# A decoder layer on one core: the cross-attention's slots regrouped, its softmax and rope steps rewritten

## Chip, cores, metric

One Trainium2 chip, one of its cores. The metric is the device time of one execution in microseconds (us), as the median of the runs. Engines: TensorE (PE, with its weight loads as PEld), VectorE (DVE), ScalarE (ACT), GpSimd (POOL), SyncE (SP, which here issues the DMAs).

## The reference, cut to what matters

The kernel computes a decoder layer for x of 64 sequences x 64 tokens x 256: causal self-attention with 16 heads, cross-attention to a context, a quantised feed-forward part, each added to x and followed by a layer norm. The change lies in the cross-attention (b = 64, lq = lk = 64, H = 16, HD = 128, R = 64):

```python
kv_c = kv @ W_kvc                      # 64 wide
q_c = q @ W_dq                         # 96 wide
q_nope = (q_c @ W_uq).reshape(b, lq, H, HD)
q_rope = _rope((q_c @ W_qr) ..., lq)   # 64 per head
k_nope, v = (kv_c @ W_uk) ..., (kv_c @ W_uv) ...
k_rope = _rope(kv_c @ W_kr, lk)
scores = (q_nope . k_nope + q_rope . k_rope) * scale
good = (k_ids <= qs) & (k_ids >= qs - LOOKBACK)
attn = softmax(where(good, scores, NEG))
return (attn @ v).reshape(b, lq, H * HD) @ W_o
```

with `_rope(x) = concat(x1*cos - x2*sin, x1*sin + x2*cos)` over the two halves of a head's 64 numbers.

## The kernel before

The 4096 tokens are handled as NT = 8 tiles of TILE = 512 (BT = 8 sequences of T = 64); the heads in HP = 8 pairs. Four blocks follow each other: self-attention (written out in full), `prepare_cross` (8 tiles; the normalised x, q_c as `qc`, the keys `kh`, kv_c by tokens as `KV`, and the weights folded so that the scores are a product of 64 + 64 numbers per head: a latent part and a rope part), the cross-attention loop, and the feed-forward part. X, the residual, stays in SBUF.

The cross-attention loop runs 64 slots, one for each head pair g and tile j: the helper `slots` writes the first 8 out, loops over the head pairs 1 to 7 with the 8 tiles inside, and adds seven slots to drain. The pair is the outer loop, the tile the inner one. Each engine has its own program; in slot n it does step k for item n - lag, `has(lag)` says whether that item exists, and semaphores join the engines. Operands are split for precision: a product of f32 numbers is three bf16 products (PASSES: high*high, high*low, low*high); the high half is read in place from the f32 tile, the low half is made by a subtraction on GpSimd or VectorE.

What a slot does, by item:

- TensorE, L889: `qP[0..2] = WQ[k].T @ qc`, 3 x 3 matmuls of 512 columns: the latent part, the rope part, and the rope part with its halves swapped (a third set of weight columns, from `in_qrs`).
- ScalarE, L934: latent part of two heads, scaled, into `qh` rows 0 to 63. VectorE, L990: `turn[0] = qP[1]*cos`, `turn[1] = qP[2]*sin`; L997: `qh` rows 64 to 127 = turn[0] + turn[1], one instruction of 64 rows for each head.
- GpSimd, L1019: `qhl`, the low half of `qh`. TensorE, L882: scores `sP`, 24 matmuls of 64 columns.
- VectorE, L983: `scores = sP + mask` (f32 mask in SBUF); L985: row maxima, negated. ScalarE, L943: eight exponentials of 64 columns, each with its row's bias and its sum.
- VectorE, L968: reciprocals of the sums; GpSimd, L1008: probs * inverse. TensorE, L896: four transposes; ScalarE, L948: `probsT` (f32).
- TensorE, L903: `oP = KV.T @ probsT`, four f32 matmuls of 128 columns. ScalarE, L928: four copies to `oT`, which bring the 64-row parts of the two heads to their rows. GpSimd, L1012: `oTl`, its low half.
- TensorE, L912: projection with `WB`, 12 matmuls of 256 columns; VectorE, L973: projP + X into X, in every slot. In the slots after the last item VectorE also takes the statistics of the 32 row blocks for the next layer norm (L542), and ScalarE sums the absolute ffn weights (L956), which SyncE loads at the loop's start (L868).

The order of work on VectorE in a slot is: reciprocal, addition into X, mask addition, maximum, two products, two sums.

The lines of the page that name L205 to L517 belong to the self-attention; `mask_of` (L389) and `square_of_tile` (L487) in it make the cross-attention's mask ahead of time, L572 is the normalisation of one block of 128 tokens in the preparation, L790 makes the low half of a folded weight there.

## Time and profile before

| | us |
|---|---|
| three runs | 1627.15, 1627.86, 1629.86; median 1627.86 |
| the profiled execution's own time | 1630.34 |
| its span, first to last instruction | 1628.5 |
| self-attention | 0 to 976 |
| preparation of the cross-attention | 976 to 1049 |
| cross-attention loop | 1049 to 1452.3 |
| quantisation, then the feed-forward loop | 1452.7 to 1492, then to 1628.5 |

Busy over the whole span: PE 1487.4 us (91%), PEld 1083.8 (67%), DVE 1322.9 (81%), ACT 1334.4 (82%), POOL 1231.7 (76%). The mean granted clock of TensorE is 0.971 of 2.4 GHz. DMA moves 36.92 MB, most of it in the first 50 us and around the preparation; there is none in most of the loop.

How to read the profile: a timeline gives instructions in order of time, neighbours of one kind merged ("x4"), with the idle time of the engine ahead of an instruction and what ended it in brackets. Two starts that lie closer than the first one's duration mean that instructions overlap in the engine's pipeline. A group by line gives the count, total and mean of a kind of instruction.

### The profile page before, as it was taken

The numbers are of one execution on the slowest core, as the hardware profiler recorded it, in microseconds if no ns is written. First come the engines' busy times: TensorE is split into PE (matmuls) and PEld (weight loads), VectorE is DVE, ScalarE is ACT, GpSimd is POOL, SyncE is SP. The second block draws the span as 40 slices with busy tenths as digits, with TensorE's granted clock in tenths as the row PEclk, the third lists the DMA queues.
The fourth block names the chain that finished last, engine by engine and source line by source line (L and its number), as shares of the span: only waits on it lengthen the run. The fifth ranks groups of instructions, "written<-read, shape, count | busy, mean of one in ns | idle before, by whom it ended". The sixth has DMA issues, their size and how long they took to land. (4 is left out here: it accounts for less than half of the span.)

```text
span 1628.5 us, 54216 instructions
## 1 busy us (share of the span) xinstructions
PE 1487.4 (91%) x20018; PEld 1083.8 (67%) x20018; DVE 1322.9 (81%) x2913; ACT 1334.4 (82%) x4174; POOL 1231.7 (76%) x1147
## 2 busy tenths in 40 slices
PE   6998999999999999999999968799999999845996
PEld 3666777777777777777777755366666666633664
DVE  3887777777777777777777778699999999967986
ACT  5877888888888888888888856599999999976664
POOL 5999888888898898898898846466666666611787
PEclk9999999999999999999999978999999999976999
DMA  6700000000000000000000002200000000000011
GB/s 222 191 2 15 16 3 15 16 15 3 15 15 3 16 15 5 13 15 15 3 15 3 3 2 68 86 3 2 0 0 0 0 0 0 0 1 0 14 39 53
DMA packets 27066, 36.92 MB, mean 23 GB/s; under 512 B 8288, under 2 KB 19872, under 8 KB 26848
## 3 DMA queue, kind: packets, MB, share of 16 engines
q1 hardware_dynamic: 26848, 33.99, 6.6%
q8 instruction: 140, 2.29, 0.5%
q14 instruction: 78, 0.64, 0.1%
HBM read 29.79 MB, written 4.19 MB: 21 GB/s over the span
## 5 line engine op out<-in xcount | busy, mean ns | idle before, releaser
L420 DVE SCALAR_TENSOR_TENSOR X<-projP,r,X 128x256 f32<-128x256 f32 x512 | 211.3, 476 | 2.5 <-PE projP L254 2.4
L234 PEld LDWEIGHTS svP<-W,xT 128*128 128x128 bf16 x3072 | 182.7, 98 | 31.4 <-issue 1.4
L205 PE MATMUL qkssP<-xT,W 128*128 128x512 bf16 x768 | 190.4, 384 | 13.5 <-POOL W L485 11.1
L480 POOL TENSOR_TENSOR y_sql<-y_sq 128x512 bf16<-128x512 f32 x128 | 133.0, 1039 | 80.5 <-ACT y_sq L321 80.1
L234 PE MATMUL svP<-W,xT 128*128 128x128 bf16 x3072 | 192.9, 219 | 0.7 <-issue 0.7
L205 PE MATMUL kP<-xT,W 128*128 128x512 bf16 x768 | 188.4, 382 | 0.0
L254 PE MATMUL projP<-W,y 128*128 128x256 bf16 x1024 | 177.1, 275 | 3.2 <-POOL yl L480 3.2
L943 ACT ACTIVATE x_probs<-x_scores,x_ntop 128x64 f32<-128x64 f32 x512 | 170.0, 335 | 7.4 <-DVE x_ntop L985 7.4
L336 ACT ACTIVATE probs<-scores,ntop 128x64 f32<-128x64 f32 x512 | 170.5, 339 | 1.9 <-DVE ntop L410 1.9
L1008 POOL TENSOR_TENSOR x_probs<-x_probs,x_inv 128x512 f32<-128x512 f32 x64 | 66.7, 1042 | 107.9 <-DVE x_inv L968 107.9
L480 POOL TENSOR_TENSOR k_sql<-k_sq 128x512 bf16<-128x512 f32 x128 | 133.1, 1040 | 19.8 <-ACT k_sq L341 19.2
L254 PE MATMUL projP<-W,yl 128*128 128x256 bf16 x512 | 140.9, 275 | 0.0
L889 PE MATMUL xq<-qc,WQ 128*128 128x512 bf16 x576 | 136.5, 383 | 3.8 <-PEq L661 2.9
L514 POOL TENSOR_TENSOR ql<-q 128x512 bf16<-128x512 f32 x128 | 139.0, 1086 | 0.0
L480 POOL TENSOR_TENSOR q_sql<-q_sq 128x512 bf16<-128x512 f32 x128 | 133.0, 1039 | 7.6 <-ACT q_sq L328 7.6
L205 PEld LDWEIGHTS kP<-xT,W 128*128 128x128 bf16 x768 | 75.7, 99 | 92.2 <-issue 2.8
L517 POOL TENSOR_TENSOR vl<-v 128x512 bf16<-128x512 f32 x128 | 135.7, 1060 | 0.0
L480 POOL TENSOR_TENSOR yl<-y 128x512 bf16<-128x512 f32 x128 | 133.0, 1039 | 0.0
L450 DVE TENSOR_TENSOR ptl<-pyP,pth 128x256 bf16<-128x256 f32 x128 | 54.3, 424 | 96.8 <-ACT pth L355 96.8
L997 DVE TENSOR_TENSOR qh<-turn 64x512 f32<-64x512 f32 x128 | 128.6, 1005 | 3.1
L1019 POOL TENSOR_TENSOR qhl<-qh 128x1024 bf16<-128x1024 f32 x64 | 121.1, 1893 | 6.2 <-DVE qh L997 6.2
L433 DVE COPY v<-svP 128x512 f32<-128x512 f32 x128 | 88.4, 691 | 44.9 <-PE svP L234 44.1
(190 smaller groups left out, 4829.1 us busy)
## 6 DMA issues: line engine op xcount, KB each, us to landing
w_stage<-in_wqkvp SPq DMA_DIRECT2D x16, 512.0 KB, 3.5
x_stage<-in_xT SPq DMA_DIRECT2D x8, 512.0 KB, 3.6
...
okv<-in_wgT SPq DMA_DIRECT2D x1, 1024.0 KB, 4.9
okv<-in_wuT SPq DMA_DIRECT2D x1, 1024.0 KB, 7.2
```

The costliest lines, as they stand in the source:

```text
L205: last = nc.tensor.matmul(dst[:, :], weight(parity, u, i, c), xT[:, z, c, tok], start=(c == 0 and k == 0), stop=(c == CC - 1 and k == 2))
L234: last = nc.tensor.matmul(svP[:, b * D:(b + 1) * D], xT[:, u, c, t * TILE + b * P:t * TILE + (b + 1) * P], weight(parity, z, 2, c), start= ...
L254: last = nc.tensor.matmul(projP[:, b * C:(b + 1) * C], y_part, W[:, (j - 3) // NT % 2, z, 3 * CC * D:], start=(i == 0), stop=(i == 2))
L336: last = nc.scalar.activation(probs[:, b, :], scores[:, b, :], ACT.Exp, bias=ntop[:, b:b + 1], accum_out=total[:, b:b + 1])
L420: last = nc.vector.scalar_tensor_tensor(acc, projP[:, b * C:(b + 1) * C], r[:, PB + b:PB + b + 1], acc, ALU.mult, ALU.add)
L480: return nc.gpsimd.tensor_tensor(dst[:, :], src[:, :], high(src, slice(None), 0, TILE), ALU.subtract)
L514: nc.gpsimd.tensor_tensor(ql[:, j % 2, :], q[:, j % 2, :], high_of(q, j % 2), ALU.subtract).then_inc(s_ql, 1)
L517: nc.gpsimd.tensor_tensor(vl[:, j % 4, :], v[:, j % 4, :], high_of(v, j % 4), ALU.subtract).then_inc(s_vl, 1)
L889: last = nc.tensor.matmul(qP[k][:, :], at(WQ[:, u, :, k], g), qc[:, z, j * TILE:(j + 1) * TILE], start=(i == 0), stop=(i == 2))
L943: last = nc.scalar.activation(probs[:, s, b, :], scores[:, b, :], ACT.Exp, bias=ntop[:, b:b + 1], accum_out=total[:, b:b + 1])
L997: last = nc.vector.tensor_tensor(qh[KVC:P, j % 2, :, i, :], turn[rows, 0], turn[rows, 1], ALU.add)
L1019: nc.gpsimd.tensor_tensor(qhl[:, s, :], flat, flat.bitcast(BF16)[:, 1::2], ALU.subtract).then_inc(s_ql, 1)
```

## The change

- The loop is written out in full and turned round: the tile is the outer loop, the head pair the inner one. The projections of a tile's eight pairs add up in PSUM (`start` only at g == 0), so `projP + X` runs once per tile; the row statistics of a tile follow in the next tile's slots.
- The third set of rope weights and its matmuls go. VectorE multiplies the rope part by -sin or sin (`turn`), SyncE moves its four blocks of 32 rows to the partner rows by four SBUF-to-SBUF DMAs (`turned`), VectorE multiplies the PSUM tile by cos in place and one slot later adds the two into `qh`. `qh` has three buffers, rope PSUM two.
- The mask is bf16 and is added by TensorE: one matmul with the identity of 512 columns opens the bank, the 24 score matmuls accumulate on it. To make the bf16 mask, self-attention uses an f32 scratch of two tiles.
- Softmax: VectorE takes the maximum from `sP`, subtracts it (`shifted`), ScalarE does one exponential of 512 columns, VectorE sums it.
- Transposed probabilities are split in bf16 (`pth` by ScalarE, `ptl` by VectorE), `KV` too (its low half by two more VectorE instructions per tile in the preparation); P times V is 12 bf16 matmuls.
- ScalarE takes `oP` to `oA` in one copy; four DMAs bring its parts to their rows (`oB`); GpSimd makes `oBl`.
- The ffn weights are loaded in slots 8 to 10. `in_ctxT` is laid out on the host so that a tile's two halves stand apart. ScalarE's load of its function table at the loop's start goes.

The diff, cut to its core:

```diff
-                m = late["mask"][:, i * BT:(i + 1) * BT, :]
                 dve.wait_ge(late["s_square"], 2 * i + 2)
-                nc.vector.tensor_scalar(m, m, (LOOKBACK / 2) ** 2, NEG, ALU.is_gt, ALU.mult)
+                nc.vector.tensor_scalar(late["mask"][:, i * BT:(i + 1) * BT, :], late["square"][:, i % 2], (LOOKBACK / 2) ** 2, NEG,
+                                        ALU.is_gt, ALU.mult).then_inc(late["s_mask"], 1)
...
-                m = late["mask"][:, i * BT:(i + 1) * BT, :]
+                m = late["square"][:, i % 2]
                 pool.wait_ge(late["s_segf"], 1)
+                wait(pool, late["s_mask"], i - 1)
...
+                if 0 <= t < NT:
+                    dve.wait_ge(s_KV, t + 1)
+                    tk, own_ = tkP[:, 0:PB * KVC].rearrange("p (b k) -> p b k", b=PB), slice(t * PB, (t + 1) * PB)
+                    nc.vector.tensor_tensor(KV[0:T, 1, own_, 0:KVC], tk[0:T], KV[0:T, 0, own_, 0:KVC], ALU.subtract)
+                    nc.vector.tensor_tensor(KV[T:P, 1, own_, KVC:P], tk[T:P], KV[T:P, 0, own_, KVC:P], ALU.subtract).then_inc(s_KVl, 1)
...
+    N = NT * HP
+    S_AT, T_AT, PV_AT, PROJ_AT = 3, 4, 5, 7
...
+            for n in range(N + PROJ_AT):
+                m = n - PV_AT - 1
+                if has(n, PV_AT + 1):
+                    wait(sp, s_oe, m + 1)
+                    wait(sp, s_proj, m - 1)
+                    for par in range(2):
+                        for i in range(2):
+                            sp.dma_start(oB[i * KVC:(i + 1) * KVC, m % 2, par * HT:(par + 1) * HT],
+                                         oA[par * KVC:(par + 1) * KVC, m % 2, i, :]).then_inc(s_ot[m % 2], 16)
+                if has(n, 0):
+                    wait(sp, s_turn, n + 1)
+                    wait(sp, s_qh, n - 1)
+                    half = R // 2
+                    for r in range(0, P, half):
+                        o = r + half if r % R == 0 else r - half
+                        sp.dma_start(turned[o:o + half, n % 2, :], turn[r:r + half, n % 2, :]).then_inc(s_swap[n % 2], 16)
+                if 8 <= n < 11:
+                    ffn_weights(n - 8, ("wgT", "wuT", "wdT")[n - 8])
...
+                if has(n, S_AT):
+                    m = n - S_AT
+                    tile, s = m // HP, m % 3
+                    wait(pe, s_ql, m + 1)
+                    wait(pe, s_shifted, m)
+                    nc.tensor.matmul(sP[:, :], identb[:, :], mask[:, tile * BT:(tile + 1) * BT, :].rearrange("p b t -> p (b t)"),
+                                     start=True, stop=False)
                     flat = qh[:, s].rearrange("p b i t -> p (b i t)")
                     for b in range(BT):
+                        first = tile * TILE + b % PB * P + b // PB * T
                         for i, (u, z) in enumerate(PASSES):
                             q_part = flat[:, b * P:(b + 1) * P].bitcast(BF16)[:, 1::2] if u == 0 else qhl[:, s, b * P:(b + 1) * P]
+                            last = nc.tensor.matmul(sP[:, b * T:(b + 1) * T], q_part, kh[:, z, first:first + T], start=False, stop=(b == BT - 1 and i == 2))
                     last.then_inc(s_s, 1)
...
+                if has(n, 0):
+                    tile, g = n // HP, n % HP
+                    for k, dst, done in ((1, ropeP[n % 2], s_ropeP), (0, latP, s_latP)):
+                        if k == 1:
+                            wait(pe, s_qh, n - 1)
+                        else:
+                            wait(pe, s_lat, n)
                         for i, (u, z) in enumerate(PASSES):
+                            last = nc.tensor.matmul(dst[:, :], WQ[:, u, g, k], qc[:, z, tile * TILE:(tile + 1) * TILE], start=(i == 0), stop=(i == 2))
+                        last.then_inc(done, 1)
...
+                if has(n, PV_AT):
+                    m = n - PV_AT
+                    wait(pe, s_ptl, m + 1)
+                    wait(pe, s_oe, m)
                     for b in range(PB):
                         for i, (u, z) in enumerate(PASSES):
+                            last = nc.tensor.matmul(oP[:, b * P:(b + 1) * P], KV[:, u, m // HP * PB + b, :], (pth, ptl)[z][:, m % 2, b * P:(b + 1) * P],
+                                                    start=(i == 0), stop=(i == 2))
+                    last.then_inc(s_o, 1)
+                if has(n, T_AT):
+                    m = n - T_AT
+                    wait(pe, s_norm, m + 1)
+                    wait(pe, s_ptl, m)
+                    for b in range(PB):
+                        last = nc.tensor.transpose(ptP[:, b * P:(b + 1) * P], probs[:, m % 2, b].rearrange("p q s -> p (q s)"), ident[:, :])
+                    last.then_inc(s_pt, 1)
...
+                if has(n, PROJ_AT):
+                    m = n - PROJ_AT
+                    g = m % HP
+                    wait(pe, s_ol, m + 1)
+                    if g == 0:
+                        wait(pe, s_acc, m // HP)
+                    for b in range(PB):
+                        for i, (u, z) in enumerate(PASSES):
+                            o_part = oB[:, m % 2, b * P:(b + 1) * P].bitcast(BF16)[:, 1::2] if u == 0 else oBl[:, m % 2, b * P:(b + 1) * P]
+                            last = nc.tensor.matmul(projP[:, b * C:(b + 1) * C], o_part, WB[:, z, g], start=(g == 0 and b % 2 == 0 and i == 0),
+                                                    stop=(g == HP - 1 and b % 2 == 1 and i == 2))
                     last.then_inc(s_proj, 1)
...
+                if has(n, S_AT):
+                    m = n - S_AT
+                    wait(act, s_shifted, m + 1)
+                    wait(act, s_pt, m - 1)
+                    nc.scalar.activation(probs[:, m % 2].rearrange("p b q s -> p q b s"), shifted[:, m % 2].rearrange("p (q b) s -> p q b s", q=2),
+                                         ACT.Exp).then_inc(s_exp, 1)
+                if has(n, T_AT):
+                    m = n - T_AT
+                    wait(act, s_pt, m + 1)
+                    wait(act, s_o, m - 1)
+                    nc.scalar.activation(pth[:, m % 2, :], ptP[:, :], ACT.Copy).then_inc(s_pth, 1)
+                if has(n, 0):
+                    wait(act, s_latP, n + 1)
+                    wait(act, s_s, n - 2)
                     for i in range(2):
+                        last = nc.scalar.activation(qh[0:KVC, n % 3, :, i, :], latP[i * KVC:(i + 1) * KVC, :].rearrange("p (b t) -> p b t", b=BT),
                                                     ACT.Copy, scale=SCALE)
                     last.then_inc(s_lat, 1)
+                if has(n, PV_AT):
+                    m = n - PV_AT
+                    wait(act, s_o, m + 1)
+                    wait(act, s_ot[m % 2], 64 * (m // 2))
+                    nc.scalar.activation(oA[:, m % 2].rearrange("p i (b t) -> p b i t", b=PB), oP[:, :].rearrange("p (b i t) -> p b i t", b=PB, i=2),
+                                         ACT.Copy).then_inc(s_oe, 1)
...
+            for n in range(N + PROJ_AT):
+                if has(n, T_AT):
+                    m = n - T_AT
+                    wait(dve, s_exp, m + 1)
+                    nc.vector.tensor_reduce(total[:, :], probs[:, m % 2].rearrange("p b q s -> p (b q) s"), AX, ALU.add).then_inc(s_sum, 1)
+                    wait(dve, s_sum, m + 1)
+                    wait(dve, s_norm, m)
                     nc.vector.reciprocal(inv[:, :], total[:, :]).then_inc(s_inv, 1)
+                if has(n, PV_AT):
+                    m = n - PV_AT
+                    wait(dve, s_pth, m + 1)
+                    wait(dve, s_o, m - 1)
+                    nc.vector.tensor_tensor(ptl[:, m % 2, :], ptP[:, :], pth[:, m % 2, :], ALU.subtract).then_inc(s_ptl, 1)
+                if has(n, S_AT):
+                    m = n - S_AT
+                    wait(dve, s_s, m + 1)
+                    nc.vector.tensor_reduce(top[:, :], by_token(sP[:, :]), AX, ALU.max).then_inc(s_top, 1)
+                    wait(dve, s_top, m + 1)
+                    wait(dve, s_exp, m - 1)
+                    nc.vector.tensor_tensor(shifted[:, m % 2], by_token(sP[:, :]), top[:, :].unsqueeze(2).to_broadcast([P, BT, T]),
+                                            ALU.subtract).then_inc(s_shifted, 1)
+                if has(n, 0):
+                    wait(dve, s_ropeP, n + 1)
+                    wait(dve, s_swap[n % 2], 64 * (n // 2))
+                    nc.vector.tensor_tensor(by_token(turn[:, n % 2]), by_token(ropeP[n % 2][:, :]), tabs[:, 1, :].unsqueeze(1).to_broadcast([P, BT, T]),
+                                            ALU.mult).then_inc(s_turn, 1)
+                if has(n, 1):
+                    m = n - 1
+                    wait(dve, s_swap[m % 2], 64 * (m // 2 + 1))
+                    wait(dve, s_cos, m + 1)
+                    wait(dve, s_s, m - 2)
                     for i in range(2):
                         rows = slice(i * R, (i + 1) * R)
+                        last = nc.vector.tensor_tensor(qh[KVC:P, m % 3, :, i, :], by_token(ropeP[m % 2][rows, :]), by_token(turned[rows, m % 2]), ALU.add)
                     last.then_inc(s_qh, 1)
+                if has(n, 0):
+                    wait(dve, s_turn, n + 1)
+                    rope = by_token(ropeP[n % 2][:, :])
+                    nc.vector.tensor_tensor(rope, rope, tabs[:, 0, :].unsqueeze(1).to_broadcast([P, BT, T]), ALU.mult).then_inc(s_cos, 1)
+                if has(n, PROJ_AT):
+                    m = n - PROJ_AT
+                    tile, g = m // HP, m % HP
+                    if g == HP - 1:
+                        wait(dve, s_proj, m + 1)
+                        acc = X[:, tile * PB:(tile + 1) * PB, :]
+                        nc.vector.tensor_tensor(acc, projP[:, :].rearrange("p (b c) -> p b c", b=PB), acc, ALU.add).then_inc(s_acc, 1)
+                    if tile >= 1 and 1 <= g < 1 + PB:
+                        wait(dve, s_acc, tile)
+                        next_norm.statistics((tile - 1) * PB + g - 1)
+            wait(dve, s_acc, NT)
+            for b in range(PB):
+                next_norm.statistics((NT - 1) * PB + b)
...
+            for n in range(N + PROJ_AT):
+                if has(n, T_AT):
+                    m = n - T_AT
+                    wait(pool, s_inv, m + 1)
+                    p_ = probs[:, m % 2].rearrange("p b q s -> p (b q) s")
                     nc.gpsimd.tensor_tensor(p_, p_, inv[:, :].unsqueeze(2).to_broadcast([P, BT, T]), ALU.mult).then_inc(s_norm, 1)
+                if has(n, PROJ_AT):
+                    m = n - PROJ_AT
+                    wait(pool, s_ot[m % 2], 64 * (m // 2 + 1))
+                    wait(pool, s_proj, m - 1)
+                    nc.gpsimd.tensor_tensor(oBl[:, m % 2, :], oB[:, m % 2, :], oB[:, m % 2, :].bitcast(BF16)[:, 1::2], ALU.subtract).then_inc(s_ol, 1)
+                if has(n, 1):
+                    m = n - 1
+                    wait(pool, s_lat, m + 1)
+                    wait(pool, s_qh, m + 1)
+                    wait(pool, s_s, m - 2)
+                    flat = qh[:, m % 3].rearrange("p b i t -> p (b i t)")
+                    nc.gpsimd.tensor_tensor(qhl[:, m % 3, :], flat, flat.bitcast(BF16)[:, 1::2], ALU.subtract).then_inc(s_ql, 1)
```

## Rows read from the trace of the kernel before

**Rows 1.** Busy us in the loop's middle: PE, PEld, DVE, ACT, POOL; granted clock, DMA share, GB/s

```profile
1085.00:1415.00 330.00, 310.19 (x3181) 220.75 (x3180) 323.67 (x446) 324.73 (x1286) 218.95 (x168) 1.00 0.00 0
```

**Rows 2.** Timeline of DVE over one slot: start us, duration us, then the instruction

```profile
1200.81 0.20 DVE L968 RECIPROCAL x_inv<-x_total 128x8 f32<-128x8 f32 x1
1200.92 1.17 DVE L973 TENSOR_TENSOR X<-xprojP,X 128x1024 f32<-128x1024 f32 x1
1202.02 0.68 DVE L983 TENSOR_TENSOR x_scores<-xsP,mask 128x512 f32<-128x512 f32 x1
1202.73 0.69 DVE L985 TENSOR_REDUCE x_ntop<-x_scores 128x8 f32<-128x512 f32 x1
1203.33 1.28 DVE L990 TENSOR_TENSOR turn<-xq,tabs 128x512 f32<-128x512 f32 x2
1204.65 1.34 DVE L997 TENSOR_TENSOR qh<-turn 64x512 f32<-64x512 f32 x1
1206.01 0.69 DVE L997 TENSOR_TENSOR qh<-turn 64x512 f32<-64x512 f32 x1
1206.73 0.20 DVE L968 RECIPROCAL x_inv<-x_total 128x8 f32<-128x8 f32 x1
```

**Rows 3.** Timeline of POOL in the same slot

```profile
1201.09 1.04 POOL L1008 TENSOR_TENSOR x_probs<-x_probs,x_inv 128x512 f32<-128x512 f32 x1 [1.56 <-DVE x_inv L968]
1203.56 1.89 POOL L1019 TENSOR_TENSOR qhl<-qh 128x1024 bf16<-128x1024 f32 x1
```

**Rows 4.** Timeline of ACT in the same slot

```profile
1200.94 1.53 ACT L928 ACTIVATE oT<-xoP 64x256 f32<-64x256 f32 x4
1202.51 1.20 ACT L934 ACTIVATE qh<-xq 64x512 f32<-64x512 f32 x2
1203.60 0.34 ACT L943 ACTIVATE x_probs<-x_scores,x_ntop 128x64 f32<-128x64 f32 x1
1206.37 0.60 ACT L948 ACTIVATE x_probsT<-xptP 128x512 f32<-128x512 f32 x1
```

**Rows 5.** Timeline of PE in the same slot, with idle time before and its releaser

```profile
1200.30 2.11 PE L889 MATMUL xq<-qc,WQ 128*128 128x512 bf16 x9
1202.68 1.08 PE L903 MATMUL xoP<-x_probsT,KV 128*128 128x128 f32 x8
1205.51 0.23 PE L882 MATMUL xsP<-kh,qh 128*128 128x64 bf16 x2 [0.37 <-POOL qhl L1019]
```

**Rows 6.** Group of instructions by line, whole span: count, busy us, mean ns, idle before

```profile
L402 DVE TENSOR_TENSOR svP<-svP,rk 128x256 f32<-128x256 f32 x128 | 54.3, 424 | 3.8 <-PE svP L280 3.8
```

**Rows 7.** DMA issues with KB and us to landing; timeline of SyncE's queue, two issues

```profile
okv<-in_wdT SPq DMA_DIRECT2D x1, 1024.0 KB, 9.6
tabs<-in_rope SPq DMA_DIRECT2D x1, 96.0 KB, 2.1
...
54.28 1.45 SPq L189 DMA_DIRECT2D kvf<-in_L_xattn_W_kvc  x1
56.92 0.43 SPq L189 DMA_DIRECT2D uqT<-in_uqT  x1
```

**Rows 8.** Timeline of DVE in the preparation, with its idle time and releaser

```profile
987.18 4.95 DVE L572 TENSOR_SCALAR X<-X,ln_mean,ln_rstd 128x256 f32<-128x256 f32 x4
1012.89 0.69 DVE L790 TENSOR_TENSOR WB<-fold,WB 128x512 bf16<-128x512 f32 x1 [0.53 <-ACT WB L760]
1014.10 3.10 DVE L572 TENSOR_SCALAR X<-X,ln_mean,ln_rstd 128x256 f32<-128x256 f32 x4
```

**Rows 9.** Timeline of DVE at the loop's start and end

```profile
1050.52 1.34 DVE L990 TENSOR_TENSOR turn<-xq,tabs 128x512 f32<-128x512 f32 x2 [3.02 <-PE xq L889]
1065.30 0.20 DVE L968 RECIPROCAL x_inv<-x_total 128x8 f32<-128x8 f32 x1
...
1421.30 4.02 DVE L542 BATCH_NORM_STATS2 ln_stats<-X 128x6 f32<-128x256 f32 x12
1450.91 1.41 DVE L542 BATCH_NORM_STATS2 ln_stats<-X 128x6 f32<-128x256 f32 x4
```

199 lines of the change are left out of this document (51 added, 148 removed).

## Prediction, before the change was run

> **What bounds the kernel now.** I read the busy table by stretch first: it shows which stage the change lives in and which engine is full there. In the cross-attention loop VectorE is busy 323.7 of 330 us and ScalarE 324.7, TensorE 310 and GpSimd 219, and TensorE's granted clock is 1.00 [rows 1]. Two engines are full, so the second reading is one slot (one head pair of one tile of 512 tokens) on each engine, as a timeline. On VectorE [rows 2] the reader is to see that each instruction starts where the one before it ends, or a little earlier, and that the reciprocal of one slot stands 5.92 us behind that of the last (1200.81 to 1206.73): 64 slots of this are 379 us. Two of its 5.92 us are the sum of the rope products, L997: the first of the pair takes 1.34, the second 0.69. The first one starts at 1204.65, while GpSimd's `qhl` runs from 1203.56 to 1205.45 [rows 3], and it ends 0.54 after that. So about 0.65 us of each slot is waiting for GpSimd. The instructions that read one operand from PSUM show nothing of the kind: the addition into X takes 1.17 beside GpSimd's `x_probs` [rows 2, 3], and the two rope products 1.28 together beside `qhl`. L997 alone reads two operands from SBUF. The Trainium skill's page "SBUF — State Buffer", section "Who interferes with whom", has it as a rule: a VectorE instruction with two SBUF inputs and a GpSimd instruction that reads SBUF wait for each other, one with a single SBUF input does not. By that rule L997 costs 0.7 once its GpSimd neighbour is out of the way, as the trace also has it.
>
> ScalarE [rows 4] is full for another reason: eight exponentials of 64 columns, each with the read-out of its sum, run from 1203.60 to 1206.37, 2.77 us, and the four parts of `oT` take 1.53. TensorE comes third and waits 0.37 for `qhl` at each slot's start [rows 5].
>
> **The change, engine by engine.** Durations overlap on VectorE, so I count from start to start. An instruction of 512 columns with a PSUM operand, or a reduction, takes 0.60 when its follower doesn't need it (1202.73 to 1203.33), and 0.71 when it does (1202.02 to 1202.73); X costs 1.09, the reciprocal 0.12 [rows 2].
>
> VectorE per slot, new order: sum of the exponentials, whose follower needs it, 0.72; reciprocal 0.12; `ptl` 0.60 (the nearest row, a subtraction from PSUM with bf16 output, L790, lasts 0.69 as the others do [rows 8]); maximum 0.72; subtraction 0.60; sine product 0.60; two sums into `qh` 1.20, since both now read one operand from PSUM; cosine product, back into PSUM, 0.60 (L402 writes to PSUM, lasts 0.42 for 256 columns [rows 6], on the same line as 0.69 for 512). Together 5.16. The maximum is taken from PSUM, which no row shows; its bounds are 0.60 (reduction from SBUF) and, if a PSUM source adds what it could at most add to a copy, about 0.80; I take 0.72. The addition into X now comes once in eight slots, and four row statistics with it: (1.09 + 4 x 0.335)/8 = 0.30, the statistics from twelve in 4.02 us [rows 9]. That makes 5.46 on average against 5.92.
>
> ScalarE: one exponential of 512 columns. A copy of that shape, L948, takes 0.60 [rows 4]; the eight small ones take 2.77. `oA` is one instruction of 0.60 too, instead of 1.53. The rest stays: 0.60 + 0.60 + 1.20 + 0.60 = 3.0 of a slot. It leaves the bound.
>
> TensorE: three of the nine wide matmuls go (the nine last 2.11 [rows 5], 0.23 each, so 0.7 less); one mask matmul of 512 columns comes (0.23); P times V goes from four f32 products in 1.08 [rows 5] to twelve bf16 ones of 128 columns, a quarter of a wide one each, 0.7. From 5.55 (5.92 less the 0.37 wait) to some 4.7.
>
> GpSimd: unchanged, two instructions of 1.04 and one of 1.89, 4.0 [rows 3]. But `qhl` of head pair n-1 now waits for the sums of the same slot, at 4.6 into it, so GpSimd runs into the next slot. I followed the ring: sums end at 4.6, `qhl` at 6.6, normalisation 7.6, `oBl` 8.6, projection on TensorE 10.1, mask and scores 11.2; the maximum that reads these scores is due at 2 x 5.16 + 1.45 = 11.8. It holds with 0.6 to spare.
>
> **The DMA detour** is what the old trace doesn't show. The swap of slot n leaves when the sine product ends, 3.4 into the slot, and the sums of the next slot want it 5.1 later. SyncE issues four transfers, about 0.48 each (issue rows run from 0.43 to 1.45 [rows 7] as the queue is free or not); the last lands 2.1 after its issue (96 KB from HBM [rows 7]). 3 x 0.48 + 2.1 + 0.2 for the two signals = 3.7. Bounds: 3.0 (issues at their shortest and a quicker landing from SBUF) and 4 x 1.45 + 2.1 = 7.9. I take 3.7, since the queue carries only 0.5 MB per slot. Then the cover is 1.4 us. Eight issues at 0.48 fill 3.8 us of SyncE's slot. The four `oT` transfers wait for ScalarE's last step of the slot before; behind that wait on SyncE stands the swap, which isn't due for another 3 us. If the cover is gone, each microsecond costs half a microsecond per slot, because a sine product waits for the sums two slots back: 2T = 5.54 + L, with L the detour and 5.54 VectorE's work between. T = 5.46 holds up to L = 5.4.
>
> **Sum.** Fill: the first rope matmuls no longer stand beside a third set, but 0.3 behind `identb`, so the first sine product comes at 1050.3 (it was 1050.52 [rows 9]); the swap lands 3.7 after its end, at 1054.7, and the sums and the cosine product close slot 1 at 1056.7. Slot 2 waits for a rope matmul (0.8, since its PSUM tile is freed by these sums) and adds 1.9 of VectorE, to 1059.4; slot 3 has the maximum and the subtraction besides, to 1063.1. So slot 4 begins at 1063, against 1065.3 [rows 9]. From there 60 slots: 60 x 5.16, seven additions into X and 24 statistics, 309.6 + 15.7 = 325, so slot 64 begins at 1388.5; before, at 1419.9 (36 slots after 1206.73). Drain: in order, the last three heads go through exponential, transposition, P times V, the `oT` detour (3.7), `oBl`, projection, X (1.2) and four statistics (1.4): 29 us, end 1417.5, where the loop before ended at 1452.3 [rows 9]. That is 34.8 less. The ffn weights, three transfers of 1 MB, now stand among the swaps of slots 8 to 10; 1.5 MB per slot against 9.6 us for 3 MB [rows 7] just about fits: +1.
>
> Preparation before the loop: two subtractions of 64x256 per tile, 0.7 us on VectorE, stand where it idles 0.53 ahead of a fold, L790 [rows 8], in most tiles; left over are 0.1 to 0.5 a tile, +1.2. `qrs` goes, and with it a GpSimd subtraction beside which four normalisations lasted 4.95 instead of 3.10 [rows 8]: -1.9. Bounds of the whole preparation: -2 and +5.6 (nothing hidden); I take -0.7. The mask now goes through two small tiles; its extra wait names a step two tiles back and costs nothing, at most 8 x 0.1 if late. The other stages are untouched.
>
> In all -34.8 + 1.0 - 0.7, about -34: the profiled execution's own time of 1630.3 becomes 1596.3. The median of the runs lies 2.5 below that execution, so 1594.
>
> **Rivals.** (a) The cover of a ring is thinner than I make it: the swap lands at 6.0, or `qhl` and what hangs on it take 1.3 us more per two slots. T becomes 5.6 to 5.8, +9 to +22 us: 1603 to 1616. For it: the ring over GpSimd has 0.6 of slack only, and signals between engines are counted at 0.1. Against: X and the statistics stretch VectorE's slots, not these rings. (b) Slower: the eight small transfers don't keep up. Price: if an issue takes 1.1 us (the row of 1.45 is such a one), SyncE needs 8.8 us per slot, 60 x 3.3 = +200, 1794; if it is the landing, L = 7.9 gives T = 6.7, +75, 1669. It decides from L = 6.5, or from 0.75 us per issue; from there the kernel is slower than before. Against: an issue beside an idle queue is 0.43 to 0.6. The Trainium skill's "SBUF — State Buffer", section "The DMA setup-cost knee", warns of just this pattern, a loop of transfers of 64 KiB, and gives it about 138 GB/s; by that, as an estimate, 0.5 MB would take 3.8 us of each slot and still fit. No row of this trace shows a transfer from SBUF to SBUF. (c) The gain is hidden: VectorE's new instructions are slower by what ends the overlap (0.70 instead of 0.60, as two SBUF operands show), eight of them, +0.8: T = 6.2, less 0.3 for what overlaps still, so 5.9, and the time stays within a few microseconds, 1625. Against: none reads two SBUF operands.
>
> **How the numbers follow.** Forecast 0.66, (a) 0.20, (b) 0.08, (c) 0.06. The forecast's own range is 1586 to 1603: VectorE's slot may be 0.1 off either way (6 us) and fill, drain and preparation 3. With (a) taken in, the range is 1584 to 1618. A measurement of this kernel tells 0.2%, 3.3 us, from no change. Faster: 0.66 + 0.20 and half of (c), 0.89; same 0.02; slower 0.09.
>
> **What would show it.** In the changed profile: two reciprocals 5.2 apart in most slots, 6.2 where X is added; VectorE over 97% busy in the loop, both sums into `qh` at 0.68 beside GpSimd; ScalarE some 3 us per slot, the one exponential 0.6; TensorE idle 0.5 to 0.8 per slot at clock 1.0; the swap landing 3.7 after its product. I am wrong if VectorE idles ahead of the sums (DMA) or of the maximum (GpSimd's ring), if the maximum from PSUM lasts over 0.8, or if TensorE's clock falls with its new idle time.

## The result, and the profile after

The changed kernel takes 1625.1 us (median of 16 runs, 1621.3 to 1629.1) against 1628.75 for the kernel before, measured beside it (16 runs): a ratio of 0.9971, 95% interval 0.9961 to 0.9981. It is faster, by 0.3%, where 2.1% was forecast. The profiled execution of the changed kernel took 1624.4 us of its own, span 1622.7, and was forecast at 1596.3.

First the page's busy table for the whole span, then the busy table by stretch for the loop's middle (PE, PEld, DVE, ACT, POOL; granted clock, DMA share, GB/s), which answers to [rows 1].

```profile
PE 1426.3 (88%) x19943; PEld 1055.6 (65%) x20146; DVE 1311.8 (81%) x3001; ACT 1136.4 (70%) x3021; POOL 1228.8 (76%) x1146
...
1081.00:1400.00 319.00, 269.62 (x3140) 192.22 (x3193) 308.61 (x519) 151.03 (x272) 212.25 (x163) 1.00 0.41 101
```

VectorE (DVE) is busy 308.6 of 319 us. ScalarE (ACT), full before, is down to 151. GpSimd ran 163 instructions, three a slot, so a slot takes 319 x 3/163 = 5.87 us on average, the share of X and its statistics included. Before, a slot took 5.92, its addition into X included [rows 2].

One slot of the changed kernel on VectorE, ScalarE, GpSimd and SyncE's queue, from timelines (start us, duration us, the instruction, in brackets the idle time before it and who ended it). These answer to [rows 2 to 4].

```profile
1207.33 0.69 DVE L1010 TENSOR_REDUCE x_total<-x_probs 128x8 f32<-128x512 f32 x1
1208.05 0.20 DVE L1013 RECIPROCAL x_inv<-x_total 128x8 f32<-128x8 f32 x1
1208.17 0.65 DVE L1018 TENSOR_TENSOR x_ptl<-xptP,x_pth 128x512 bf16<-128x512 f32 x1
1208.74 0.68 DVE L1022 TENSOR_REDUCE x_top<-xsP 128x8 f32<-128x512 f32 x1
1209.45 0.69 DVE L1025 TENSOR_TENSOR x_shifted<-xsP,x_top 128x512 f32<-128x512 f32 x1
1210.06 0.68 DVE L1030 TENSOR_TENSOR x_turn<-xropeP,tabs 128x512 f32<-128x512 f32 x1
1210.77 1.39 DVE L1039 TENSOR_TENSOR qh<-xropeP,x_turned 64x512 f32<-64x512 f32 x2
1212.20 0.70 DVE L1044 TENSOR_TENSOR xropeP<-xropeP,tabs 128x512 f32<-128x512 f32 x1
1212.93 0.69 DVE L1010 TENSOR_REDUCE x_total<-x_probs 128x8 f32<-128x512 f32 x1
...
1210.18 0.63 ACT L972 ACTIVATE x_probs<-x_shifted 128x512 f32<-128x512 f32 x1 [2.78 <-DVE x_shifted L1025]
1210.71 0.58 ACT L978 ACTIVATE x_pth<-xptP 128x512 bf16<-128x512 f32 x1
1211.19 1.18 ACT L983 ACTIVATE qh<-xlatP 64x512 f32<-64x512 f32 x2
...
1206.70 1.89 POOL L1078 TENSOR_TENSOR qhl<-qh 128x1024 bf16<-128x1024 f32 x1 [1.93 <-issue]
1208.55 1.04 POOL L1066 TENSOR_TENSOR x_probs<-x_probs,x_inv 128x512 f32<-128x512 f32 x1
1209.55 1.04 POOL L1071 TENSOR_TENSOR oBl<-oB 128x512 bf16<-128x512 f32 x1
...
1205.17 2.45 SPq L903 DMA_DIRECT2D x_turned<-x_turn  x4
1207.72 2.46 SPq L895 DMA_DIRECT2D oB<-oA  x4
```

VectorE is back to back, as forecast, but the slot from L1010 to L1010 is 5.60 us and not 5.16. Counted from start to start, up to the sine product every step is what the sum said, within 0.03: 0.72, 0.12, 0.57, 0.71, 0.61. Then four starts are late: sine product to first sum 0.71, first to second sum 0.70 (the pair lasts 1.39), second sum to cosine product 0.73, cosine product to the next slot's L1010 0.73. The sum had 0.60 for each, 2.40; they take 2.87. That is 0.47 too much; the other steps give 0.03 back, and 0.44 is left.

ScalarE, GpSimd and SyncE all have slack: ScalarE waits 2.78 us for `x_shifted`, GpSimd 1.93 ahead of `qhl`. SyncE has the least: counted issue by issue from 1081 to 1380, the idle stretches of its queue that are longer than 0.15 us add up to 22.4 us of 299, 0.4 us a slot. VectorE's wait for the swap in these 319 us, from the table of waits, and the two new transfers in the table of DMA issues (KB, median us to landing):

```profile
DVE qh L1039 <- DMA x_turned<-x_turn: 0.9, 2, 0.6
...
x_turned<-x_turn SPq DMA_DIRECT2D x256, 64.0 KB, 2.0
oB<-oA SPq DMA_DIRECT2D x256, 64.0 KB, 2.0
```

The loop's start and its end on VectorE, which answer to [rows 9]:

```profile
1048.03 0.69 DVE L1030 TENSOR_TENSOR x_turn<-xropeP,tabs 128x512 f32<-128x512 f32 x1 [2.73 <-PE xropeP L933]
...
1414.19 0.69 DVE L1010 TENSOR_REDUCE x_total<-x_probs 128x8 f32<-128x512 f32 x1
...
1443.50 1.23 DVE L1051 TENSOR_TENSOR X<-xprojP,X 128x1024 f32<-128x1024 f32 x1 [12.23 <-PE xprojP L960]
1444.76 1.40 DVE L543 BATCH_NORM_STATS2 ln_stats<-X 128x6 f32<-128x256 f32 x4
```

Slot 4 begins at 1062.3 (forecast 1063), slot 64 at 1414.2 (1388.5), the loop ends at 1446.2 (1417.5). So 60 slots took 351.9 us instead of 325, and this is where the gain went. The drain is 32.0 instead of 29.

### The profile page after: what moved, and what is told of

Same layout as the page of the kernel before. It is cut to its first block and busy times, and to the rows that moved or that the text cites. A ratio compares the mean times of both kernels' runs of the same rounds, so it can differ in the third digit from the quotient of the medians.

```text
span 1622.7 us, 53246 instructions
## 1 busy us (share of the span) xinstructions
PE 1426.3 (88%) x19943; PEld 1055.6 (65%) x20146; DVE 1311.8 (81%) x3001; ACT 1136.4 (70%) x3021; POOL 1228.8 (76%) x1146
## 5 line engine op out<-in xcount | busy, mean ns | idle before, releaser
L205 PE MATMUL qkssP<-xT,W 128*128 128x512 bf16 x641 | 160.9, 382 | 33.6 <-issue 20.3
L972 ACT ACTIVATE x_probs<-x_shifted 128x512 f32<-128x512 f32 x64 | 40.3, 630 | 191.4 <-DVE x_shifted L1025 191.4
L450 DVE TENSOR_TENSOR ptl<-pyP,pth 128x256 bf16<-128x256 f32 x128 | 54.3, 424 | 96.8 <-ACT pth L355 96.8
L205 PEld LDWEIGHTS qkssP<-xT,W 128*128 128x128 bf16 x768 | 64.9, 98 | 81.5 <-issue 12.3
L407 DVE SCALAR_TENSOR_TENSOR scores<-svP,r,bias 128x64 f32<-128x64 f32 x512 | 110.0, 278 | 4.5
L960 PE MATMUL xprojP<-WB,oB 128*128 128x256 bf16 x512 | 89.2, 276 | 25.5 <-POOL oBl L1071 25.5
```

What stands on the lines that cost most here:

```text
L205: last = nc.tensor.matmul(dst[:, :], weight(parity, u, i, c), xT[:, z, c, tok], start=(c == 0 and k == 0), stop=(c == CC - 1 and k == 2))
L407: last = nc.vector.scalar_tensor_tensor(scores[:, b, :], svP[:, b * T:(b + 1) * T], r[:, b:b + 1], row, ALU.mult, ALU.add)
L960: last = nc.tensor.matmul(projP[:, b * C:(b + 1) * C], o_part, WB[:, z, g], start=(g == 0 and b % 2 == 0 and i == 0), stop=(g == HP - 1 an ...
```

## The experiments

The question is why four starts in each slot are 0.10 to 0.13 late. Theory A: a VectorE instruction overlaps the tail of the one in front of it only if it starts at the partitions that were last used in that memory, for reading and for writing. (A memory here is SBUF or PSUM.) The rivals are B, the waits and the transfer ahead of the sums; C, the 64-row shape or the output in PSUM; D, GpSimd at the port. Behind each measured time stands its ratio to the kernel before, measured beside it, with the 95% interval; the changed kernel's is 0.9971. The kernel before took 1628.75 to 1632.5 from one series to the next, so versions of different series are compared by these ratios.

**The sums turned round.**

```
-                    for i in range(2):
+                    for i in (1, 0):
```

> The changed kernel with one thing turned round: of a slot's two 64-row sums, the one that reads rows 64 to 127 is issued first. Work, tiles, waits and engines are the same. Theory A (a VectorE instruction does not overlap the one in front of it when it starts to read PSUM, to read SBUF or to write SBUF at another partition than was last used there): in the changed kernel four starts of a slot pay, the first sum (output from row 64), the second (inputs from row 64), the cosine product (inputs back at row 0) and the instruction behind it (SBUF output back at row 0): 0.71, 0.70, 0.73 and 0.73 us from start to start, where other 512-element instructions take 0.57 to 0.61. Turned round, the second sum ends on rows 0 to 63, where the cosine product reads: it should start 0.60 to 0.62 us behind the sum instead of 0.73, the slot fall from 5.60 to 5.48, the kernel by 64 x 0.12 = 7 to 8 us, ratio to the kernel before 0.992 to 0.993. The Trainium skill, VectorE: DVE Perf Modes, section Two Vector instructions with no wait between them, has this as its condition for a held instruction. Theory B (three waits ahead of the sums, or the transfer that feeds them), theory C (a 64-row instruction or one that writes PSUM costs more in itself) and theory D (GpSimd's traffic at the same port): the order changes nothing, slot 5.60, ratio 0.997.

Measured: 1618.8 us, 0.9933 (0.9913 to 0.9953). VectorE's timeline:

```profile
1204.29 0.68 DVE L1030 TENSOR_TENSOR x_turn<-xropeP,tabs 128x512 f32<-128x512 f32 x1
1205.00 1.39 DVE L1039 TENSOR_TENSOR qh<-xropeP,x_turned 64x512 f32<-64x512 f32 x2
1206.32 0.68 DVE L1044 TENSOR_TENSOR xropeP<-xropeP,tabs 128x512 f32<-128x512 f32 x1
1207.03 0.69 DVE L1010 TENSOR_REDUCE x_total<-x_probs 128x8 f32<-128x512 f32 x1
...
1212.50 0.69 DVE L1010 TENSOR_REDUCE x_total<-x_probs 128x8 f32<-128x512 f32 x1
```

The pair still lasts 1.39, but the cosine product starts 1.32 behind it instead of 1.43; the slot is 5.47. Nothing but the order differs, so of the rivals none explains it; a 64-row sum isn't slow in itself, since the second one now holds its follower for 0.61 only. 6 us are won by letting the second sum end where the next instruction reads.

**The sums on all 128 rows** (their result left out from the fourth slot on).

```
+                            last = nc.vector.tensor_tensor(late["square"][:, :].rearrange("p i b t -> p (i b t)").rearrange("p (b i t) -> p b i t", b=BT, i=2)[:, :, i, :], by_token(ropeP[m % 2][:, :]), by_token(turned[:, m % 2]), ALU.add)
```

> The changed kernel, but from the fourth slot on the two sums are made on all 128 rows, from row 0, into a tile that nobody reads, so the rope part of the queries keeps old values: the result of the sums is left out, not their work. Each sum still has 512 elements a row, the same waits and the same order. Theory A (starting partition): no instruction of the slot leaves row 0, so the two sums, the cosine product and what follows it all start 0.58 to 0.61 us behind the one before; the slot goes from 5.60 to 5.16 us and the kernel from 1625 to about 1597 us (61 slots x 0.44 = 27 us), the time forecast, ratio about 0.980. Theory B (waits or the transfer): the first sum still starts 0.71 behind the sine product, slot 5.5 at best. Theory C: with the 64-row shape as the cause both sums take 0.60 but the cosine product, which has 128 rows in both kernels, still 0.73 if its PSUM output is what costs there: slot 5.3, 1607 us. Theory D (GpSimd at the port): sums unchanged at 0.70, slot 5.60, 1625 us.

Measured: 1603.7 us, 0.9837 (0.9812 to 0.9863).

```profile
1209.10 0.68 DVE L1030 TENSOR_TENSOR x_turn<-xropeP,tabs 128x512 f32<-128x512 f32 x1
1209.70 1.28 DVE L1042 TENSOR_TENSOR square<-xropeP,x_turned 128x512 f32<-128x512 f32 x2
1210.89 0.69 DVE L1047 TENSOR_TENSOR xropeP<-xropeP,tabs 128x512 f32<-128x512 f32 x1
1211.49 1.21 DVE L1054 TENSOR_TENSOR X<-xprojP,X 128x1024 f32<-128x1024 f32 x1
...
DVE square L1042 <- DMA x_turned<-x_turn: 8.4, 11, 1.8
```

All four starts are at 0.60: 0.60, 1.19 for the pair, 0.60. Where nobody waits, one reciprocal follows another by 5.11 (1113.84 to 1118.95), so the forecast's 5.16 was the slot of a kernel that never leaves row 0. The elements a row and the waits are the same, and the cosine product still writes PSUM: B, D and that half of C fall. From 1075 to 1385 the first sum starts 0.59 to 0.60 behind the sine product in 38 of 58 slots, and later in the others, of which the table of waits puts 11 down to the swap. So 21 us come back and not 27: the last line, from the table of waits, has 8.4 us of VectorE waiting for the swap, against 0.9 in the changed kernel. SyncE's queue is full here: its idle stretches over 0.15 us add up to 1.7 us of 299, and a round of eight issues takes 5.53 us on average. The average slot, X's share included, can't be shorter than that here.

**The three waits moved ahead of the sine product.**

```
+                if has(n, 1):
+                    wait(dve, s_swap[(n - 1) % 2], 64 * ((n - 1) // 2 + 1))
+                    wait(dve, s_cos, n)
+                    wait(dve, s_s, n - 3)
                 if has(n, 0):
                     wait(dve, s_ropeP, n + 1)
```

> The changed kernel with the three waits of the two sums (for the transfer, for the cosine product of the slot before and for the buffer) moved ahead of the sine product, so that nothing stands between the sine product and the sums. Theory A (starting partition): the starts stay at 0.71, 0.70, 0.73 and 0.73 us, slot 5.60, time within 1 us of the changed kernel, ratio 0.997; a loss of up to 0.2 us a slot is possible if the transfer of the slot before is not yet in at the earlier point (then 1630 to 1638 us). Theory B (the three waits cost the time in which the instruction could have overlapped): first sum 0.60 behind the sine product, slot 5.49, 7 us shorter, ratio 0.993.

Measured: 1626.6 us, 0.9981 (0.9967 to 0.9996).

```profile
1206.60 0.68 DVE L1034 TENSOR_TENSOR x_turn<-xropeP,tabs 128x512 f32<-128x512 f32 x1
1207.31 1.39 DVE L1040 TENSOR_TENSOR qh<-xropeP,x_turned 64x512 f32<-64x512 f32 x2
```

Still 0.71 with nothing between the two. B is out.

**The cosine product in SBUF, behind the sine product.**

```
+                    nc.vector.tensor_tensor(by_token(cosd[:, n % 2]), by_token(ropeP[n % 2][:, :]), tabs[:, 0, :].unsqueeze(1).to_broadcast([P, BT, T]),
+                                            ALU.mult).then_inc(s_cos, 1)
...
-                        last = nc.vector.tensor_tensor(qh[KVC:P, m % 3, :, i, :], by_token(ropeP[m % 2][rows, :]), by_token(turned[rows, m % 2]), ALU.add)
+                        last = nc.vector.tensor_tensor(qh[KVC:P, m % 3, :, i, :], by_token(cosd[rows, m % 2]), by_token(turned[rows, m % 2]), ALU.add)
```

> The changed kernel, but the cosine product goes to an SBUF tile, right behind the sine product, instead of back into PSUM behind the sums; the sums then read two SBUF tiles. Both products start at row 0 for reading and writing. Theory A (starting partition): three starts of a slot pay, the first sum, the second sum and the instruction behind it, the cosine product does not: 0.60 for the cosine product behind the sine product, 0.70 for each sum and 0.73 for what follows; slot 5.48, 7 us shorter than the changed kernel, ratio 0.992 to 0.993. Theory C (writing PSUM costs 0.13 us): cosine product 0.60, its follower no longer pays either: slot 5.35, 1610 us. Theory D (two SBUF operands run against GpSimd at a shared port, which the traces so far do not exclude: in the kernel before, the first of the two sums, both of whose operands lie in SBUF, took 1.34 us beside GpSimd's pass): each sum may take up to 1.3 us while GpSimd runs, slot up to 6.7 us, and the kernel up to 70 us longer; a ratio over 1.00 shows it.

Measured: 1616.7 us, 0.9923 (0.9898 to 0.9948).

```profile
1206.39 0.68 DVE L1031 TENSOR_TENSOR x_turn<-xropeP,tabs 128x512 f32<-128x512 f32 x1
1206.99 0.68 DVE L1034 TENSOR_TENSOR square<-xropeP,tabs 128x512 f32<-128x512 f32 x1
1207.70 1.39 DVE L1043 TENSOR_TENSOR qh<-square,x_turned 64x512 f32<-64x512 f32 x2
1209.12 0.69 DVE L1011 TENSOR_REDUCE x_total<-x_probs 128x8 f32<-128x512 f32 x1
```

0.60 for the cosine product, 0.71 to the first sum, 1.42 for the pair: slot 5.46, three late starts, as theory A had it. C, by which its follower too would be quicker, falls. D isn't tested here: GpSimd's `qhl` starts at 1209.22, behind the sums.

**The port, in the kernel before.** Its sums' first operand goes to PSUM.

```
+                        dst = qP[1][:, :].rearrange("p (b t) -> p b t", b=BT) if k == 0 else turn[:, k]
-                        last = nc.vector.tensor_tensor(turn[:, k], qP[1 + k][:, :].rearrange("p (b t) -> p b t", b=BT),
+                        last = nc.vector.tensor_tensor(dst, qP[1 + k][:, :].rearrange("p (b t) -> p b t", b=BT),
...
-                        last = nc.vector.tensor_tensor(qh[KVC:P, j % 2, :, i, :], turn[rows, 0], turn[rows, 1], ALU.add)
+                        last = nc.vector.tensor_tensor(qh[KVC:P, j % 2, :, i, :], qP[1][rows, :].rearrange("p (b t) -> p b t", b=BT), turn[rows, 1], ALU.add)
```

> The kernel before with one edit: the cosine product is written back into its PSUM tile, so that the two sums into qh read one operand from PSUM and one from SBUF, beside GpSimd's qhl as before. The prediction took the 1.34 us of the first sum for 0.69 of work and 0.65 of waiting for GpSimd, because both operands lie in SBUF. Then the first sum should now last 0.69 to 0.71 beside qhl, VectorE's work of a slot fall from 5.92 to about 5.3, and the time hardly change, because ScalarE, 324.7 of 330 us busy, bounds at 5.83 to 5.9: 0 to 5 us shorter, ratio 0.997 to 1.000. If the 1.34 had another cause (the dependence on the product in front of it), the first sum stays at 1.3 and VectorE's slot at 5.9.

Measured: 1629.2 us, 0.9988 (0.9970 to 1.0005), no difference. VectorE's sums and GpSimd's `qhl` beside them:

```profile
1211.18 1.39 DVE L1000 TENSOR_TENSOR qh<-xq,turn 64x512 f32<-64x512 f32 x2
...
1210.27 1.89 POOL L1022 TENSOR_TENSOR qhl<-qh 128x1024 bf16<-128x1024 f32 x1
```

The pair lasts 1.39 beside `qhl` in all 50 slots from 1081 to 1380, where it was 1.34 + 0.69 [rows 2]. VectorE's busy time in 330 us falls from 323.7 [rows 1] to 294.0, and the time stays, since ScalarE is busy 324.8. The prediction's reading of the 1.34 us was right.

**The parts of the change alone.** The addition into X in every slot:

```
-                    if g == 0:
-                        wait(pe, s_acc, m // HP)
+                    wait(pe, s_acc, m)
...
-                    if g == HP - 1:
+                    if True:
```

> The changed kernel without the summing in PSUM: each head pair's projection is added into X by VectorE, as in the kernel before (1.14 us a time), with the other parts of the change kept. If VectorE bounds and X's addition is all cost on it (main theory): seven more additions in eight slots, 7/8 x 1.14 = 1.0 us a slot, 60 us or a little more in all: 1683 to 1690 us, ratio 1.034 to 1.038. If part of X's addition would lie in time that the slot has anyway, less: 1650 to 1670. It measures what the PSUM part of the change is worth in this kernel, as the run with ScalarE's softmax measures the softmax part.

Measured: 1688.9 us, 1.0352 (1.0322 to 1.0383). Summing in PSUM is worth 62 us (by the ratios) to 64 (by the medians) to the changed kernel; 56 additions of 1.14 are 64.

The softmax back on ScalarE:

```
+                    for b in range(BT):
+                        col = b % PB * 2 + b // PB
+                        last = nc.scalar.activation(probs[:, m % 2, b % PB, b // PB, :], sP[:, b * T:(b + 1) * T], ACT.Exp,
+                                                    bias=top[:, b:b + 1], accum_out=total[:, col:col + 1])
```

> The changed kernel with its softmax put back on ScalarE alone: eight exponentials a slot straight from PSUM, with the negated maximum as bias and their sums read out by ScalarE; the subtraction (0.61 us) and the sum over the exponentials (0.72) leave VectorE. Everything else of the change stays. If VectorE's row of instructions is what sets the slot (main theory), it falls to 5.60 - 1.33 = 4.27 and ScalarE becomes the bound with 2.77 (eight exponentials) + 0.6 (pth) + 1.2 (qh) + 0.6 (oA) = 5.05 to 5.2 us a slot; against 5.92 on average with X's addition that is 60 x 0.75 to 0.85, 45 to 50 us shorter: 1573 to 1582 us, ratio 0.966 to 0.971. If one of the rings (the swap by DMA, or GpSimd's chain to the next scores) is about to bound at the slot now measured, the gain stops early: VectorE idles ahead of the sums or of the maximum, slot 5.4 or more, 1600 us or more.

Measured: 1607.2 us, 0.9843 (0.9812 to 0.9874). Undoing this part makes the kernel 18 us faster by the medians, 21 by the ratios: with the four-part copies gone, ScalarE had room for its exponentials, and VectorE had none for 1.33 us more. But 45 to 50 were expected. The table of waits (299 us of the loop) and SyncE's queue:

```profile
DVE qh L1036 <- DMA x_turned<-x_turn: 60.8, 48, 3.2
...
1199.71 3.77 SPq L893 DMA_DIRECT2D oB<-oA  x4
1203.58 2.44 SPq L901 DMA_DIRECT2D x_turned<-x_turn  x4
1206.12 2.46 SPq L893 DMA_DIRECT2D oB<-oA  x4
1208.68 2.44 SPq L901 DMA_DIRECT2D x_turned<-x_turn  x4
```

The sine product to be swapped began at 1204.37, but its transfers are issued from 1208.68: the queue was still at `oB`, which stands ahead. Eight issues of 0.61 and the waits fill 5.1 us, and not all are so short: in the group at 1199.71 one issue takes 1.95 us and the four 3.77. From 1081 to 1380, 23 of 430 issues take over 0.8 us. The mean round is 5.56 us, and the queue is idle for more than 0.15 us at a time in 5.6 us of 299 only. So the queue sets the slot in this version, and VectorE's softmax may cost more than the 18 to 21 us that show here. What makes one issue in 18 a long one, no run shows.

**Is it the queue?** The same bytes in twelve issues a slot instead of eight:

```
+                        for c in (0, TILE // 2):
+                            sp.dma_start(turned[o:o + half, n % 2, c:c + TILE // 2], turn[r:r + half, n % 2, c:c + TILE // 2]).then_inc(s_swap[n % 2], 16)
```

> The changed kernel with each of the four swap transfers cut into two of half the columns: the same bytes, twelve issues a slot on SyncE instead of eight. It tests the slower rival's mechanism, the queue of small transfers. If an issue holds SyncE for about 0.61 us whatever its size, as the rows of the changed kernel have it (four in 2.45), twelve take 7.35 and with the waits 7.5 to 7.7 us a slot, 2 us more than 5.6: 1720 to 1740 us. If the issue's time follows its bytes (half as long for half the columns), nothing changes, 1625 us.

Measured: 1757.2 us (one run).

```profile
1204.48 5.91 SPq L904 DMA_DIRECT2D x_turned<-x_turn  x8
1210.49 2.45 SPq L895 DMA_DIRECT2D oB<-oA  x4
1213.05 5.23 SPq L904 DMA_DIRECT2D x_turned<-x_turn  x8
```

An issue of half the bytes takes no less: the median is 0.59 us, as for a whole one in the changed kernel. The round from 1204.48 to 1213.05 takes 8.57 us, one long issue of 1.5 us in it; the mean round from 1081 to 1380 is 8.08, and the kernel's slot follows it (5.87 + (1757.2 - 1625.1)/60 = 8.07). That is more than the 7.5 to 7.7 expected, and the time lies above the 1720 to 1740: the expectation had no long issues, which add 0.4 us a round. The slower rival's mechanism is real. The changed kernel stands some 0.4 us a slot from it.

**A version to beat both**: softmax on ScalarE, cosine product in SBUF, two score tiles.

```
-    latP, ropeP = ps("xlatP"), [ps("xropeP0"), ps("xropeP1")]
-    sP, ptP, oP = ps("xsP"), ps("xptP"), ps("xoP")
+    latP, ropeP = ps("xlatP"), ps("xropeP")
+    sP2, ptP, oP = [ps("xsP0"), ps("xsP1")], ps("xptP"), ps("xoP")
```

> A version to beat both kernels: softmax by ScalarE's eight exponentials from PSUM (subtraction and sum leave VectorE), the cosine product to SBUF right behind the sine product, one rope tile in PSUM instead of two, the scores' tile doubled instead. VectorE has 0.72 + 0.12 + 0.70 + 0.60 + 0.60 + 0.70 + 0.70 = 4.1 us a slot and 0.3 for X, ScalarE 5.05 to 5.2: ScalarE bounds, slot 5.05 to 5.2, 1566 to 1580 us, ratio 0.962 to 0.970, within 5 us of the version that only has its softmax on ScalarE. If in that one the single scores' tile had made TensorE or VectorE wait, this one is the faster of the two by up to 15 us.

Measured: 1603.1 us, 0.9831 (0.9800 to 0.9861), the lowest median of the kernels that compute everything, but not told apart from the version with its softmax on ScalarE alone (0.9812 to 0.9874), and again not the 1566 to 1580 expected. VectorE still waits 43.9 us of 299 for the swap, SyncE's queue is as full as there (idle for 4.0 us of 299, mean round 5.57), and now the two-SBUF-operand sums meet GpSimd:

```profile
1202.09 2.26 DVE L1043 TENSOR_TENSOR qh<-square,x_turned 64x512 f32<-64x512 f32 x2 [0.43 <-DMA x_turned<-x_turn]
...
1202.06 1.04 POOL L1071 TENSOR_TENSOR oBl<-oB 128x512 bf16<-128x512 f32 x1
```

2.26 instead of 1.39 for the pair, the longest one. From 1081 to 1380 it lasts 1.39 in all 22 slots where GpSimd is idle beside it, and 1.39 to 2.26 in the 31 others. This is theory D's effect.

**ScalarE issues the `oB` transfers**, to relieve SyncE, in that version and in one that splits the softmax by slots.

```
-                            sp.dma_start(oB[i * KVC:(i + 1) * KVC, m % 2, par * HT:(par + 1) * HT],
+                            act.dma_start(oB[i * KVC:(i + 1) * KVC, m % 2, par * HT:(par + 1) * HT],
                                          oA[par * KVC:(par + 1) * KVC, m % 2, i, :]).then_inc(s_ot[m % 2], 16)
```

> The combined version (softmax on ScalarE, cosine product to SBUF, two scores' tiles) with the four oB transfers of a slot issued by ScalarE at the start of its next slot instead of by SyncE. In the two versions with the softmax on ScalarE, SyncE issued two groups of four transfers back to back, 2.44 and 2.46 us long, and VectorE waited 44 to 61 us for the swap; the slot came out at 5.4 us instead of the 5.05 to 5.2 forecast. Theory Q (SyncE's queue is the bound there): with half of its issues gone the wait for the swap falls under 10 us and the slot to ScalarE's own row, 5.05 us plus what four issues cost on ScalarE: if 0.1 each, slot 5.2 to 5.3, 1585 to 1592 us, ratio 0.971 to 0.976; if an issue holds ScalarE for 0.6, as it does SyncE, the slot is 7.3 and the kernel 1720 us. Theory R (the transfers' landing or GpSimd's ring is the bound): time unchanged within 3 us of 1603, VectorE's wait for the swap stays.

> The changed kernel with the cosine product in SBUF, the softmax by VectorE subtraction, one exponential and a VectorE sum in the even slots and by eight exponentials on ScalarE in the odd ones, and the oB transfers issued by ScalarE. Two slots cost VectorE 2 x 5.46 - 1.33 = 9.6 us, 4.8 a slot, with X 5.1; ScalarE (5.05 + 3.0)/2 = 4.0 plus four issues, 4.4 if an issue costs 0.1; SyncE 2.5; TensorE 4.7. Main theory: VectorE's row bounds, average slot 5.1 to 5.2, against 5.46 + 0.3 for the cosine version: 60 x 0.6 = 36 us below 1617, 1581 to 1590 us, ratio 0.970 to 0.976. If the alternation makes each engine wait for the other's long slot, 1600 or more.

Measured: 1723.6 us, 1.0567 (1.0531 to 1.0604), and 1670.9 us, 1.0238 (1.0214 to 1.0261). ScalarE's queue in the first:

```profile
1196.72 2.42 ACTq L966 DMA_DIRECT2D oB<-oA  x4
...
1203.94 3.61 ACTq L966 DMA_DIRECT2D oB<-oA  x4
1207.67 0.32 ACT L976 ACTIVATE x_probs<-xsP,x_top 128x64 f32<-128x64 f32 x1 [3.77 <-issue]
```

An issue holds ScalarE for 0.6 us (median 0.62 of 157 from 1081 to 1380), as it does SyncE; the second group has a long one of 1.55 us in it. The slot follows: GpSimd ran 117 instructions in 290 us, 7.4 us a slot, and the 1720 us written down for 0.6 us an issue came true. VectorE's wait for the swap is gone from the table of waits, as theory Q had it, but the bound has moved to ScalarE. The split version misses its 1581 to 1590 for the same reason: it had counted 0.1 us an issue. With 4 x 0.6 ScalarE's row is 4.0 + 2.4 = 6.4 us a slot, and the slot is 6.6.

**The split with all transfers on SyncE again:**

```
+                    if m % 2 == 0:
+                        wait(act, s_shifted, m // 2 + 1)
...
+                    else:
+                        wait(act, s_top, m + 1)
+                        wait(act, s_inv, m)
+                        for b in range(BT):
...
```

> The version that splits the softmax by slots (even slots by VectorE's subtraction and sum, odd slots by eight exponentials on ScalarE, cosine product in SBUF), now with all eight transfers of a slot issued by SyncE again, since four issues on ScalarE held it for 3.1 to 3.6 us. VectorE's row comes to 4.8 us a slot and 5.1 with X, ScalarE's to 4.0, SyncE's queue to 2.44 + 2.46 + 0.2 = 5.1. If only these rows bound, the average slot is 5.1 to 5.3, 1585 to 1600 us, ratio 0.972 to 0.982, and it beats the version that had all of its softmax on ScalarE (1603 us). If SyncE's queue costs more than its issues, because the oB transfers stand ahead of the swap in it and wait for ScalarE's last step, VectorE waits for the swap again, slot 5.4, 1600 to 1608 us.

Measured: 1609.4 us, 0.9873 (0.9844 to 0.9901). VectorE waits 19.7 us for the swap in 299 and is busy 266.6. SyncE's queue is full again: it is idle for more than 0.15 us at a time in 5.0 us of 299, its mean round is 5.59, and no slot can be shorter on average. That is just above the 1600 to 1608 expected for this case, which had 5.4.

## Why the prediction was wrong

**The step that failed** is the counting rule: "takes 0.60 when its follower doesn't need it (1202.73 to 1203.33), and 0.71 when it does", and with it the terms "two sums into `qh` 1.20" and "cosine product 0.60", and the 0.60 ahead of the first sum. Need is one cause of a late start (0.71 and 0.72 in the changed kernel too), but it isn't the only one, and none of these four late starts comes from it. The rule fitted [rows 2] in two places, but the same group had a row against it: the second L997 starts at 1206.01 and the reciprocal behind it, which doesn't need it, at 1206.73, 0.72 later. The second cause is a change of the rows at which the instructions start. The runs show this as A: order alone moves 0.13 of a slot, and keeping to row 0 moves 0.49. The Trainium skill states the rule on "VectorE: DVE Perf Modes", section "Two Vector instructions with no wait between them": an instruction whose input or output starts in another group of 32 partitions than the last one in that memory starts only when all earlier ones have finished. The trace agrees, at 0.10 to 0.13 us for 512 columns here; the loop's instructions move by 64 rows only, so a move by 32 isn't tested. The rows of the changed kernel part output from input. The first sum reads from row 0, as the sine product did, and moves only its output, to row 64: 0.71. The second sum moves only its inputs: 0.70. And the position is kept for each memory by itself: the cosine product writes PSUM between the second sum and L1010, yet L1010, whose output goes back to row 0 of SBUF, starts 0.73 behind it; with nothing in SBUF off row 0 it is 0.60. Whether a move in PSUM alone holds a start wasn't run.

**In size**: 60 slots x 0.44 = 26.4 us of the 28.1 that the profiled execution is above its forecast.

**A second term was mis-sized, and hidden by the first**: "Eight issues at 0.48 fill 3.8 us of SyncE's slot". They fill 5.0 us, 5.5 with gaps and waits (the round of 5.53 in the run on 128 rows, where the queue is full). The forecast's average slot is 325/60 = 5.42, just under that. So with its counting right the kernel would still have missed 1594: the run on 128 rows, with 5.11 for the 5.16, took 1603.7.

**Rival (c)** had the result to the microsecond, 1625, and its cause by half. It had 0.70 instead of 0.60 "by what ends the overlap", but on eight instructions, tied to two SBUF operands, and then took back 0.3. Four starts are late and none of the instructions has two SBUF operands. That 0.8 - 0.3 comes so near to the 0.47 measured is luck. It got 0.06 where the row at 1206.73 should have raised it.

**What was right**: ScalarE's fall to 3 us a slot (151.0/54.3 = 2.8); the maximum straight from PSUM at 0.72 (0.71); X and statistics, 15.7 us over the 60 slots (351.9 - 60 x 5.60 = 15.9); the first sum's 1.34 us as a matter of GpSimd and operands; the swap as hidden, at 3.7 us (by the rows after, 3 x 0.61 + 2.0 + 0.2 = 4.0).

**What was off by less**: the drain, 32.0 for 29, where X waits 12.2 us for TensorE and the chain ahead of it; the preparation, 71.0 us before and 68.0 after, 3.1 less where 0.7 was forecast, outside the bound of -2 that it was given; the start of slot 4, 1062.3 for 1063, right by luck, since the first sine product came 2.3 us earlier than forecast and the way from there took 14.3 us and not 12.7; an issue on SyncE at 0.61 for 0.48, which made the slack against rival (b) 0.14 us an issue and not 0.27, before long issues are counted; TensorE at 269.6/54.3 = 5.0 us a slot for 4.7. The last sum is off by 0.5 in itself: -34.8 + 1.0 - 0.7 is -34.5, so 1595.8 and not 1596.3.

**Rival (a)** named rings that didn't bind at 5.60. At 5.11 VectorE waited for the swap, 8.4 us in 319, but what set the slot there was SyncE's queue, which rival (b) names, and not a landing or GpSimd's ring.
